# Output product of an attention stage: four half-precision products per 128 tokens, or two single-precision products of 64 tokens

## The chip, the cores and the metric

The kernel runs on one core of a Trainium2 chip. The metric is the device time of one execution in microseconds (us); the figure before the change is the median of three runs.

## The reference

The reference takes 16 sequences of 512 tokens of 128 channels. It normalizes each token (xn), and then computes two things from xn: a recurrent attention, and a mixture of eight experts with a shared expert beside them. The result is x + s * silu(g), where s is the attention's output and g the mixture's.

The attention has 16 heads of 8 channels. Tokens are mixed with their predecessors and projected to r, k and v. Within a chunk, y is the product of r and k of all earlier tokens, weighted with a decay, times v; from the chunks before comes r times a state that is carried on with k and v. Its last step is `out = y @ Wo.T + bo`, with Wo of 128 x 128: this is the product that is changed. Inputs, weights and outputs are single precision.

## The kernel before

The kernel has two long stages. The first normalizes, routes, computes the experts and the projections of r and k, and ends at about 555 us of the span. The second is the attention and the final gating.

The attention is worked off in 16 units (NA = 16). A unit `u` is 128 tokens of four sequences, so 512 columns, in two chunks of Q = 64 tokens (CH = 2) per sequence; a half `p` of a unit is two sequences. Every engine has a program of its own with a loop over `u`, written out by hand and skewed against the others: in one turn of the loop the engine works on unit `u` for one step and on `u - 1` or `u - 2` for another. Semaphores tie them together, and each engine takes its instructions in order.

TensorE (PE) in one turn (lines 1743 to 1760): `pe_local` of the second half of `u - 1` (r times k, L1672), `pe_inter` of `u - 1` (state times r, L1652), `pe_av` of its first half (L1693), `pe_out` of `u - 2` (the output product, L1704 to L1707), `pe_kv` and `pe_local` of `u` in three pieces (L1614, L1616, L1621 and L1672), `pe_av` of the second half of `u - 1` (L1693), and `pe_update` of `u` (k times v for the state, L1636).

VectorE (DVE) in one turn: `dve_select` gathers y of a half from the result of `pe_av` and adds the part of the state (L1321, four instructions a half), `dve_state` carries the state on (L1292, two a unit), and `dve_decay` weights r times k (L1303, four a unit). The selected y stands in `y32` in single precision; its columns are ordered by half, chunk, sequence and token.

The output product takes half-precision operands. For that y is split. `act_high` on ScalarE (ACT) rounds a half of `y32` to `yh` (L864), and `pool_low` on GpSimd (POOL) computes `yl = y32 - yh` (L670); for the last unit VectorE does this (`dve_low_last`, L1338). Both also put the columns in plain token order. The weights Wo stand as a pair, too, in slot 6 of `wph` and `wpl`. `pe_out` waits for `y_lo` (both low halves of the unit) and for the state of unit `u + 1`, since it writes to a PSUM bank that the update of the state also uses. Then, for each of four blocks of 128 tokens, it adds four products of 128 x 128: the bias (`f2y` times `brw`), `yh` with the high weights, `yh` with the low weights, and `yl` with the high weights. The last unit goes through `pe_out_last`, by halves, and its gating (L1345) and final sum (L1352) are done on VectorE, behind the gating of the unit before (L1330).

GpSimd's turn begins with the two `pool_low`; behind them stand a mask of the state (L663) for unit `u + 2`, the final sum of `u - 2` (L698), two additions of the experts' rows (L677, L682), the gating (L688), and the mask for unit `u + 1`, which `pe_inter` waits for. ScalarE's turn holds `act_high` of the first half behind the copies of k and v (L843), and of the second half between the masks of r (L857) and the weighting of the experts' rows (L872).

Before `dve_select` overwrites `y32` of unit `u - 2`, it waits for its low halves (`y_lo`).

Of the kernel before, what the change touches and what calls it, by code (L numbers as in the profile page):

```python
# [7 lines left out]
F32, F16, I32 = mybir.dt.float32, mybir.dt.float16, mybir.dt.int32  # L8
ALU = mybir.AluOpType
# [3 lines left out]
P = 128  # L13
HEADS, HD = 16, 8
Q = 64
CH = P // Q
GROUP = 32
GROUPS = P // GROUP
HPG = GROUP // HD
# [11 lines left out]
SW = 2.0 ** 8  # L31
# [38 lines left out]
def build(nc, nb, x, decay, per_head, maa, wT, bias, bias_rows, gateT, w1e, w3e, w2e, w1s, w3s, w2s, const, out):  # L70
# [8 lines left out]
    NA = TPS * NG  # L79
# [9 lines left out]
    with ctx:  # L89
        def sb(name, shape, dt=F32):  # L90
            return ctx.enter_context(nc.sbuf_tensor(name, shape, dt))
# [28 lines left out]
        sem = Semaphores()  # L120
# [19 lines left out]
        take = carve(ffn[:, 0:NT // 2, :].rearrange("p a b -> p (a b)"))  # L140
# [20 lines left out]
        take = carve(hidden[:, :])  # L161
# [63 lines left out]
        mx = sb("mx", [P, 3])  # L225
        omx = sb("omx", [P, 3])
        w32 = late([P, 4, P])
        ws32 = late([P, 7, P])
        wph = sb("wph", [P, 7, P], F16)
        wpl = sb("wpl", [P, 7, P], F16)  # L230
        brk = sb("brk", [P, 2])
        brs = sb("brs", [P, 2])
        bro = late([P, 3 * P])
# [29 lines left out]
        a32 = take([P, 2, GROUPS, 2 * HPG * Q])  # L263
        yint = take([P, 2, 512])
        y32 = take([P, 2, 512])
        yh = take([P, 2, 512], F16)
        yl = take([P, 2, 512], F16)
        st = [first_state, take([P, NG, 4 * HALF])]
        sm = take([P, 4, 4 * HALF])
        picked = [take([P, PRING, 4, P]) for k in range(2)]  # L270
# [83 lines left out]
            v = a[:, 4 * g * TPS:4 * (g + 1) * TPS]  # L354
            return v.rearrange("p (b t) d -> p b t d", t=TPS)[:, :, tt, :]

        def by_chunk(a, u, p):
            return a[:, u % 2, 2 * p * P:2 * (p + 1) * P].rearrange("p (c b i) -> p b c i", c=CH, b=2)

        def in_order(a, u, p):  # L360
            return a[:, u % 2, 2 * p * P:2 * (p + 1) * P].rearrange("p (b c i) -> p b c i", c=CH, b=2)

        NHOTS = 2 * NT
        HOT_FIRST, HOT_SLOTS, HOT_LAG = 13, 24, 3
# [64 lines left out]
        def at(u):  # L429
            return 0 <= u < NA  # L430
# [173 lines left out]
        def pool_program(e):  # L604
# [59 lines left out]
                                st[c][:, g, :].rearrange("p (b d) -> p b d", b=4),  # L664
                                rep_mid(C("head"), 4), ALU.mult).then_inc(sem[f"masked{c}"], 1)

            def pool_low(n):
                u, p = divmod(n, 2)
                G.wait_ge(sem["y_hi"], n + 1)
                G.tensor_tensor(in_order(yl, u, p), by_chunk(y32, u, p), in_order(yh, u, p), ALU.subtract).then_inc(sem["y_lo"], 1)  # L670

            def pool_add(u, step):
                p0 = picked[0][:, u % PRING, :, :]
                if step == 0:
# [37 lines left out]
                    pool_scatter(q - SCATTER_LAG)  # L712
            pool_state0()
            for u in range(-2, NA + 3):
                if at(u - 1) and u - 1 < NA - 1:
                    pool_low(2 * (u - 1))
                    pool_low(2 * (u - 1) + 1)
                if at(u + 2):
                    pool_mask(2 * (u + 2))
                if at(u - 2) and u - 2 < NA - 3:  # L720
                    pool_end(u - 2)
                if at(u):
                    pool_add(u, 0)
                    pool_add(u, 1)
                if at(u - 1) and u - 1 < NA - 2:
                    pool_gate(u - 1)
                if at(u + 1):
                    pool_mask(2 * (u + 1) + 1)
                if u - 1 in (NA - 3, NA - 2):
                    pool_end(u - 1)  # L730

        @block.scalar
        def act_program(e):
# [122 lines left out]
                    A.wait_ge(sem["local"], 2 * (u - 1))  # L856
                A.mul(rm[:, u % 2, q, :], r32[:, u % RRING, :], C("slot")[:, q:q + 1]).then_inc(sem[f"rmask{q // 2 * 2}"], 1)  # L857

            def act_high(n):
                u, p = divmod(n, 2)  # L860
                A.wait_ge(sem["ysel"], HPG * (n + 1))
                if u >= 2 and p == 0:
                    A.wait_ge(sem["s_out"], u - 1)
                A.copy(in_order(yh, u, p), by_chunk(y32, u, p)).then_inc(sem["y_hi"], 1)  # L864

            def act_weigh(u, k):
                A.wait_ge(sem[f"picked{u % PRING}"], 32 * (u // PRING + 1))
                if u == 0:
# [54 lines left out]
            for u in range(-2, NA + 3):  # L923
                if at(u - 1):
                    act_weigh(u - 1, 0)
                if at(u - 2) and u - 2 < NA - 2:
                    act_out(u - 2)
                if at(u):
                    act_kv(u, 0)
                    act_kv(u, 1)  # L930
                if at(u - 1):
                    act_high(2 * (u - 1))
# [8 lines left out]
                if at(u - 1):  # L941
                    act_high(2 * (u - 1) + 1)
                if at(u):
                    act_weigh(u, 1)
                    act_inter(u)

        @block.vector
        def dve_program(e):
# [298 lines left out]
            def dve_proj_weights(i):  # L1247

                if i == 1:
                    V.wait_ge(sem["late_in"], 48)  # L1250
                    V.wait_ge(sem["mixes"], 1)
                    V.tensor_scalar(ws32[:, 6, :], w32[:, 3, :], SW, None, ALU.mult).then_inc(sem["aconst"], 1)
                V.tensor_scalar(ws32[:, i, :], w32[:, i, :], omx[:, i:i + 1], SW, ALU.mult, ALU.mult).then_inc(sem["aconst"], 1)
                V.tensor_scalar(ws32[:, 3 + i, :], w32[:, i, :], mx[:, i:i + 1], SW, ALU.mult, ALU.mult).then_inc(sem["aconst"], 1)

            def dve_proj_pair(step):

                V.wait_ge(sem["aconst"], 8 + 2 * step)
                for some in (slice(1, 3), slice(4, 7)):
                    if step == 0:  # L1260
                        V.tensor_copy(wph[:, some, :], ws32[:, some, :]).then_inc(sem["aconst"], 1)
                    else:
                        V.tensor_tensor(wpl[:, some, :], ws32[:, some, :], wph[:, some, :], ALU.subtract).then_inc(sem["aconst"], 1)
# [41 lines left out]
            def dve_select(n, heads):  # L1305
                u, p = divmod(n, 2)
                if heads[0] == 0:
                    V.wait_ge(sem["av"], n + 1)
                    V.wait_ge(sem["yint"], u + 1)
                    if u >= 2 and p == 0:  # L1310
                        V.wait_ge(sem["y_lo"], 2 * (u - 1))

                def pair(a):
                    return a[:, u % 2, 2 * p * P:2 * (p + 1) * P].rearrange("p (a i) -> p a i", i=Q)

                for q in heads:
                    if q > 0:
                        V.wait_ge(sem["ysel"], HPG * n + q)
                    first = av_bank(n)
                    y = banks[:, first:first + 2, :].rearrange("p c (b q i) -> p (c b) q i", b=2, q=HPG)[:, :, q, :]  # L1320
                    V.scalar_tensor_tensor(pair(y32), y, C("slot_y")[:, q:q + 1], pair(y32 if q else yint),  # L1321
                                           ALU.mult, ALU.add).then_inc(sem["ysel"], 1)

            def dve_gate(u):
# [8 lines left out]
            def dve_low_last(p):  # L1333
                u = NA - 1
                V.wait_ge(sem["y_hi"], 2 * u + p + 1)
                if p == 0:
                    V.wait_ge(sem["s_out"], u - 1)
                V.tensor_tensor(in_order(yl, u, p), by_chunk(y32, u, p), in_order(yh, u, p), ALU.subtract).then_inc(sem["y_lo_last"], 1)  # L1338

            def dve_gate_last(p):  # L1340
                V.wait_ge(sem["out_last"], p + 1)
# [84 lines left out]
            for u in range(-2, NA + 3):  # L1426
# [11 lines left out]
                if at(u + 2):  # L1438
                    dve_decay(2 * (u + 2), 1)
                    dve_decay(2 * (u + 2), 0)  # L1440
            for p in range(2):
                dve_low_last(p)
            dve_gate(NA - 2)
            for p in range(2):
                dve_gate_last(p)
# [3 lines left out]
        def pe_program(e):  # L1449
# [245 lines left out]
                k.then_inc(sem["av"], 1)  # L1695

            def pe_out(u):
                T.wait_ge(sem["y_lo"], 2 * (u + 1))
                T.wait_ge(sem["state"], 2 * (u + 2))
                s = u % 2  # L1700
                for b in range(4):
                    o = psum[1][:, b * P:(b + 1) * P]
                    X = slice(b * P, (b + 1) * P)
                    T.matmul(o, f2y[:, :], brw[:, 2 * P:3 * P], start=True, stop=False)  # L1704
                    T.matmul(o, yh[:, s, X], wph[:, 6, :], start=False, stop=False)
                    T.matmul(o, yh[:, s, X], wpl[:, 6, :], start=False, stop=False)
                    k = T.matmul(o, yl[:, s, X], wph[:, 6, :], start=False, stop=True)  # L1707
                k.then_inc(sem["s_out"], 1)

            def pe_out_last(p):  # L1710
                T.wait_ge(sem["y_lo_last"], p + 1)
                s = (NA - 1) % 2
                for b in range(2):
                    o = psum[4 + p][:, b * P:(b + 1) * P]
                    X = slice((2 * p + b) * P, (2 * p + b + 1) * P)
                    T.matmul(o, f2y[:, :], brw[:, 2 * P:3 * P], start=True, stop=False)
                    T.matmul(o, yh[:, s, X], wph[:, 6, :], start=False, stop=False)
                    T.matmul(o, yh[:, s, X], wpl[:, 6, :], start=False, stop=False)
                    k = T.matmul(o, yl[:, s, X], wph[:, 6, :], start=False, stop=True)
                k.then_inc(sem["out_last"], 1)  # L1720

            for b in range(nb + 2):
# [67 lines left out]
```

## Time and profile before

| what | value |
|---|---|
| median of three runs | 721.59 us (720.73 to 722.53) |
| span of the profiled execution, from its first to its last instruction | 719.3 us |
| TensorE busy | 654.1 us, 91% |
| VectorE busy | 555.4 us, 77% |
| ScalarE busy | 494.9 us, 69% |
| GpSimd busy | 478.9 us, 67% |
| attention stage | from about 555 us to the end of the span |

The profiled execution's own time is known by its span alone: 719.3 us, from its first to its last instruction; the median of the timed runs stands 2.3 us above it. Busy shares are means over both stages. The start of a matmul is recorded and its end is modelled, so a matmul that overlaps the one before it counts as busy twice over; the rows below are read by starts.

### The profile page before, as it was taken

To read this page: it belongs to the slowest core of one execution; us is meant where nothing else is said; L and a number is where in the kernel's file an instruction comes from. 1 tells how busy PE (TensorE), PEld (TensorE's weight loads), DVE (VectorE), ACT (ScalarE), POOL (GpSimd) and SP (SyncE) were. 2 spreads that over 40 slices of the span, in tenths; PEclk is the share of its full clock that TensorE was granted. 3 is DMA by queue.
4 is the path that set the end of the run, shared out by engine and by line. 5 is a ranking of instruction groups with operands and counts; after the bars stand their busy time and mean duration, and the time that the engine had idled before them with its cause. 6 is when DMAs were issued, how large, how long until landed. Compare 5 with 4: busy or idle time off the path is not lost.

```text
span 719.3 us, 22370 instructions
## 1 busy us (share of the span) xinstructions
PE 654.1 (91%) x8536; PEld 452.1 (63%) x8536; DVE 555.4 (77%) x1058; ACT 494.9 (69%) x1008; POOL 478.9 (67%) x519
## 2 busy tenths in 40 slices
PE   2787897978999999999999999999997899999993
PEld 1544565646665665566666666878886676777772
DVE  5989986877667886667766676667664899999996
ACT  4864798857665656666666666666665788888872
POOL 4844321244777777777777777767778487888873
PEclk9999999999999999999999999999999999999997
DMA  9931111111111323433323334333362767777762
GB/s 243 299 95 45 45 61 46 45 51 36 48 49 49 108 91 108 137 108 108 110 92 109 106 106 139 110 101 108 97 103 93 237 179 230 216 229 222 233 176 59
DMA packets 88616, 86.75 MB, mean 121 GB/s; under 512 B 11394, under 2 KB 65284, under 8 KB 88516
## 3 DMA queue, kind: packets, MB, share of 16 engines
q1 hardware_dynamic: 79428, 66.70, 29.8%
q0 software_dynamic: 9088, 18.63, 9.6%
q8 instruction: 73, 1.20, 0.7%
q14 instruction: 27, 0.22, 0.1%
HBM read 50.82 MB, written 34.47 MB: 119 GB/s over the span
## 4 chain that ended last, share of the span: by engine, by line
PE 53%; DVE 13%; ACT 12%; POOL 11%; issue 7%; DMA 3%; SPq 0%; POOLq 0%; DVEq 0%; ACTq 0%
PE banks L1556 7%; PE banks L1558 7%; PE banks L1557 7%; PE banks L1596 5%; DVE hidden L1218 4%; POOL expert_rows L644 4%; PE banks L1576 4%; PE banks L1577 4%; PE banks L1575 4%; POOL srows L634 3%; ACT hidden L785 3%; PE banks L1621 3%; PE banks L1693 3%; PE banks L1672 3%; ACT rows L823 2%
## 5 line engine op out<-in xcount | busy, mean ns | idle before, releaser
L785 ACT CAST hidden<-hidden 128x512 f16<-128x512 f32 x206 | 127.1, 617 | 135.5 <-DVE hidden L1218 135.4
L634 POOL DMA_INDIRECT srows<-normed_rows,source x142 | 149.7, 1054 | 60.4 <-issue 40.2
L1222 DVE TENSOR_TENSOR hidden<-hidden 128x512 f16<-128x512 f32 x180 | 124.4, 691 | 83.9 <-ACT hidden L785 83.0
L1218 DVE TENSOR_TENSOR hidden<-hidden,banks 128x512 f32<-128x512 f32 x206 | 140.8, 684 | 44.0 <-ACT hidden L781 38.2
L1575 PE MATMUL banks<-wwords,hidden 128*128 (+1 forms) x824 | 148.8, 219 | 1.5 <-DVE hidden L1222 1.1
L1576 PE MATMUL banks<-wwords,hidden 128*128 (+1 forms) x824 | 148.6, 219 | 0.0
L1577 PE MATMUL banks<-wwords,hidden 128*128 (+1 forms) x824 | 148.6, 219 | 0.0
L781 ACT ACTIVATE hidden<-banks 128x512 f32<-128x512 f32 x206 | 122.7, 596 | 28.1 <-PE banks L1558 27.8
L1556 PE MATMUL banks<-sx,wwords 128*128 128x512 f16 (+1 forms) x368 | 121.5, 330 | 3.2 <-DVE wwords L1013 2.7
L1558 PE MATMUL banks<-sx,wwords 128*128 128x512 f16 (+1 forms) x368 | 121.6, 330 | 0.0
L1557 PE MATMUL banks<-sx,wwords 128*128 128x512 f16 (+1 forms) x368 | 121.5, 330 | 0.0
L644 POOL DMA_INDIRECT expert_rows<-ybuf,dest x72 | 77.2, 1072 | 22.8 <-issue 19.8
L1575 PEld LDWEIGHTS banks<-wwords,hidden 128*128 128x128 f16 x824 | 80.6, 98 | 12.4 <-issue 2.0
L644 POOL DMA_INDIRECT expert_rows<-rows,dest x70 | 72.8, 1040 | 23.1 <-issue 20.1
L1576 PEld LDWEIGHTS banks<-wwords,hidden 128*128 128x128 f16 x824 | 80.6, 98 | 11.3
L624 POOL TENSOR_TENSOR hidden<-hidden 128x512 f16<-128x512 f32 x26 | 33.6, 1294 | 76.8 <-ACT hidden L785 76.8
L1303 DVE TENSOR_TENSOR wwords<-banks,wmat 128x1024 f32<-128x1024 f32 x64 | 75.3, 1217 | 10.9 <-PE banks L1672 10.5
L1577 PEld LDWEIGHTS banks<-wwords,hidden 128*128 128x128 f16 x824 | 80.6, 98 | 0.0
L1556 PE MATMUL banks<-xh,wwords 128*128 128x512 f16 x128 | 49.2, 385 | 19.1 <-DVE hidden L1218 18.7
L1321 DVE SCALAR_TENSOR_TENSOR hidden<-banks,cst,hidden 128x256 f32<-128x256 f32 x128 | 61.5, 481 | 3.8 <-ACT hidden L849 0.7
L1558 PEld LDWEIGHTS banks<-sx,wwords 128*128 x368 | 36.0, 98 | 25.6
L1557 PE MATMUL banks<-xl,wwords 128*128 128x512 f16 x128 | 49.0, 383 | 0.0
(218 smaller groups left out, 1429.7 us busy)
## 6 DMA issues: line engine op xcount, KB each, us to landing
rows<-x SPq DMA_DIRECT2D x32, 256.0 KB, 4.9
rows<-expert_rows SPq DMA_DIRECT2D x32, 256.0 KB, 3.6
normed_rows<-rows SPq DMA_DIRECT2D x16, 256.0 KB, 3.9
r_rows<-rows SPq DMA_DIRECT2D x16, 256.0 KB, 2.1
rd_rows<-rows SPq DMA_DIRECT2D x16, 256.0 KB, 2.2
stage<-r_rows SPq DMA_DIRECT2D x16, 256.0 KB, 4.0
k_rows<-rows SPq DMA_DIRECT2D x16, 256.0 KB, 2.2
kd_rows<-rows SPq DMA_DIRECT2D x16, 256.0 KB, 2.2
```

The source lines that it names most:

```text
L634: G.indirect_dma_start(srows[:, q % NXB, t, :], None, rows_in, bass.IndirectOffsetOnAxis(source[:, at:at + 1], 0)).then_inc(sem[f"s_in{q % ...
L644: G.indirect_dma_start(rows_out, bass.IndirectOffsetOnAxis(dest[:, at:at + 1], 0), ring_of(q)[:, t, :], None).then_inc(sem[f"y_stored{q % ...
L781: A.activation(sg[:, i % 2, :], psum[2 * (i % 2)][:, :], ACT.Silu, scale=1.0 / SW).then_inc(sem["silu"], 1)
L785: A.copy(guh[:, i % 4, :], gu[:, i % 2, :]).then_inc(sem["gu_hi"], 1)
L1218: V.tensor_tensor(gu[:, i % 2, :], sg[:, i % 2, :], psum[2 * (i % 2) + 1][:, :], ALU.mult).then_inc(sem["gated"], 1)
L1222: V.tensor_tensor(gul[:, i % 4, :], gu[:, i % 2, :], guh[:, i % 4, :], ALU.subtract).then_inc(sem["gu_lo"], 1)
L1556: T.matmul(o, a, mh, start=True, stop=False)
L1557: T.matmul(o, a, ml, start=False, stop=False)
L1558: k = T.matmul(o, b, mh, start=False, stop=True)
L1575: T.matmul(o, guh[:, i % 4, s], a, start=(j == 0 and n == 0), stop=False)
L1576: T.matmul(o, guh[:, i % 4, s], b, start=False, stop=False)
L1577: k = T.matmul(o, gul[:, i % 4, s], a, start=False, stop=last)
```

## The change

The pair of y is gone: `yh` and `yl`, `act_high`, `pool_low` and `dve_low_last` with their places in the three loops, and slot 6 of `wph` and `wpl`. `pe_out` waits for the selections of y themselves (`ysel`), and takes `y32` and single-precision weights `wo32`. In a block of 128 tokens the bias is added as before, and then two products follow, each with 64 columns of `y32` (one chunk of one sequence) as the stationary operand and the 128 columns of `wo32` as the moving one; the first writes partitions 0 to 63 of the block's result, the second partitions 64 to 127. `dve_select` waits for the output product of unit `u - 2` (`s_out`) in place of its low halves.

```diff
-        wph = sb("wph", [P, 7, P], F16)
-        wpl = sb("wpl", [P, 7, P], F16)
+        wph = sb("wph", [P, 6, P], F16)
+        wpl = sb("wpl", [P, 6, P], F16)
+        wo32 = sb("wo32", [P, P])
...
+        def piece(a, u, b, c):
+            at = b // 2 * 2 * P + c * P + b % 2 * Q
+            return a[:, u % 2, at:at + Q]
...
-            def pool_low(n):
-                u, p = divmod(n, 2)
-                G.wait_ge(sem["y_hi"], n + 1)
-                G.tensor_tensor(in_order(yl, u, p), by_chunk(y32, u, p), in_order(yh, u, p), ALU.subtract).then_inc(sem["y_lo"], 1)
...
-            def act_high(n):
-                u, p = divmod(n, 2)
-                A.wait_ge(sem["ysel"], HPG * (n + 1))
-                if u >= 2 and p == 0:
-                    A.wait_ge(sem["s_out"], u - 1)
-                A.copy(in_order(yh, u, p), by_chunk(y32, u, p)).then_inc(sem["y_hi"], 1)
...
-                    V.tensor_scalar(ws32[:, 6, :], w32[:, 3, :], SW, None, ALU.mult).then_inc(sem["aconst"], 1)
+                    V.tensor_scalar(wo32[:, :], w32[:, 3, :], SW, None, ALU.mult).then_inc(sem["aconst"], 1)
...
-                for some in (slice(1, 3), slice(4, 7)):
+                for some in (slice(1, 3), slice(4, 6)):
...
-                        V.wait_ge(sem["y_lo"], 2 * (u - 1))
+                        V.wait_ge(sem["s_out"], u - 1)
...
-            for p in range(2):
-                dve_low_last(p)
...
             def pe_out(u):
-                T.wait_ge(sem["y_lo"], 2 * (u + 1))
+                T.wait_ge(sem["ysel"], HPG * 2 * (u + 1))
                 T.wait_ge(sem["state"], 2 * (u + 2))
-                s = u % 2
                 for b in range(4):
                     o = psum[1][:, b * P:(b + 1) * P]
-                    X = slice(b * P, (b + 1) * P)
                     T.matmul(o, f2y[:, :], brw[:, 2 * P:3 * P], start=True, stop=False)
-                    T.matmul(o, yh[:, s, X], wph[:, 6, :], start=False, stop=False)
-                    T.matmul(o, yh[:, s, X], wpl[:, 6, :], start=False, stop=False)
-                    k = T.matmul(o, yl[:, s, X], wph[:, 6, :], start=False, stop=True)
+                    for c in range(CH):
+                        k = T.matmul(o[c * Q:(c + 1) * Q, :], piece(y32, u, b, c), wo32[:, :], start=False, stop=True)
                 k.then_inc(sem["s_out"], 1)
```

`pe_out_last` is changed in the same way, and waits for the selections of its half.

## Rows read from the trace of the kernel before

**Rows 1.** Stretches: two units' length; PE, PEld, DVE, ACT, POOL busy, clock, DMA.
```profile
core 0: us, PE busy (x) PEld busy (x) DVE busy (x) ACT busy (x) POOL busy (x), PEclk, DMA share, GB/s
634.76:644.10 9.34, 9.20 (x255) 6.77 (x248) 9.09 (x16) 7.94 (x20) 7.77 (x9) 1.00 0.73 215
644.10:653.44 9.34, 9.20 (x255) 6.77 (x248) 9.09 (x16) 7.95 (x20) 7.77 (x9) 1.00 0.82 244
```

**Rows 2.** Waits of VectorE, 572 to 700 us: total, times, longest.
```profile
DVE wwords L1303 <- PE banks L1672: 1.2, 3, 0.6
DVE hidden L1321 <- PE banks L1693: 0.2, 1, 0.2
DVE hidden L1292 <- PE banks L1636: 0.2, 1, 0.2
```

**Rows 3.** Timeline of one turn: start, length, instruction, count, idle before.
```profile
645.02 1.52 DVE L1321 SCALAR_TENSOR_TENSOR hidden<-banks,cst,hidden 128x256 f32<-128x256 f32 x3
645.50 1.15 PE L1652 MATMUL banks<-wwords,rows 64*64 64x64 f32 x32
646.45 0.47 DVE L1292 SCALAR_TENSOR_TENSOR stage<-hidden,ws,banks 128x256 f32<-128x256 f32 x1
646.68 1.10 PE L1693 MATMUL banks<-wwords 64*32 64x256 f32 x32
646.68 0.39 ACT L864 CAST wwords<-hidden 128x256 f16<-128x256 f32 x1
647.15 0.68 POOL L670 TENSOR_TENSOR hidden<-hidden,wwords 128x256 f16<-128x256 f32 x1 [0.61 <-ACT wwords L864]
647.89 0.23 PE L1704 MATMUL banks<-brw,f2y 128*128 128x128 f16 x1
647.95 0.22 PE L1705 MATMUL banks<-wph,wwords 128*128 128x128 f16 x1
...
648.79 0.32 PE L1614 MATMUL banks<-cst,wwords 128*128 128x128 f32 x1
...
649.34 0.28 PE L1614 MATMUL banks<-cst,wwords 128*128 128x128 f32 x1
649.45 0.22 PE L1616 MATMUL banks<-brw,f 128*128 128x128 f16 x1
...
649.73 0.22 PE L1621 MATMUL banks<-wpl,xh 128*128 128x128 f16 x1
649.79 0.22 PE L1621 MATMUL banks<-wph,xl 128*128 128x128 f16 x1
649.94 1.12 PE L1672 MATMUL banks<-wwords,rows 32*64 32x256 f32 x32
650.99 0.33 PE L1614 MATMUL banks<-cst,wwords 128*128 128x128 f32 x1
...
652.14 1.09 PE L1693 MATMUL banks<-wwords 64*32 64x256 f32 x32
653.17 0.69 PE L1636 MATMUL banks<-wwords 64*64 64x64 f32 x32
653.79 1.12 PE L1672 MATMUL banks<-wwords,rows 32*64 32x256 f32 x32
```

**Rows 4.** Groups of instructions, 572 to 704 us: count, busy, mean ns, idle before.
```profile
L1704 PE MATMUL banks<-brw,f2y 128*128 128x128 f16 x56 | 12.4, 222 | 1.2
```

**Rows 5.** Timeline of TensorE where L1652 begins: its first pair, then two pairs.
```profile
645.50 0.27 PE L1652 MATMUL banks<-wwords,rows 64*64 64x64 f32 x2
...
645.50 0.33 PE L1652 MATMUL banks<-wwords,rows 64*64 64x64 f32 x4
```

**Rows 6.** Timeline of TensorE ahead of one other output product.
```profile
589.85 1.55 PE L1693 MATMUL banks<-wwords 64*32 64x256 f32 x32
591.33 0.23 PE L1704 MATMUL banks<-brw,f2y 128*128 128x128 f16 x1
```

**Rows 7.** Timeline of VectorE at the end of the span.
```profile
705.42 3.98 DVE L1321 SCALAR_TENSOR_TENSOR hidden<-banks,cst,hidden 128x256 f32<-128x256 f32 x8
709.32 0.98 DVE L1338 TENSOR_TENSOR hidden<-hidden,wwords 128x256 f16<-128x256 f32 x2
710.22 0.68 DVE L1330 SCALAR_TENSOR_TENSOR rows<-banks,rows 128x512 f32<-128x512 f32 x1
```

**Rows 8.** Stretches at the end of the span, columns as in rows 1.
```profile
700.00:710.00 10.00, 6.36 (x188) 4.33 (x180) 9.53 (x19) 5.29 (x15) 6.29 (x7) 0.95 0.19 54
710.00:719.30 9.30, 1.68 (x16) 1.41 (x14) 3.25 (x6) 0.00 (x0) 1.26 (x1) 0.50 0.20 56
```

More of the change, by code:

```diff
@@ L227, in build @@
         w32 = late([P, 4, P])
-        ws32 = late([P, 7, P])
-        wph = sb("wph", [P, 7, P], F16)
-        wpl = sb("wpl", [P, 7, P], F16)
+        ws32 = late([P, 6, P])
+        wph = sb("wph", [P, 6, P], F16)
+        wpl = sb("wpl", [P, 6, P], F16)
+        wo32 = sb("wo32", [P, P])
         brk = sb("brk", [P, 2])
@@ L265, in build @@
         y32 = take([P, 2, 512])
-        yh = take([P, 2, 512], F16)
-        yl = take([P, 2, 512], F16)
         st = [first_state, take([P, NG, 4 * HALF])]
@@ L714, in pool_program @@
             for u in range(-2, NA + 3):
-                if at(u - 1) and u - 1 < NA - 1:
-                    pool_low(2 * (u - 1))
-                    pool_low(2 * (u - 1) + 1)
                 if at(u + 2):
@@ L930, in act_program @@
                     act_kv(u, 1)
-                if at(u - 1):
-                    act_high(2 * (u - 1))
                 if at(u + 1):
@@ L940, in act_program @@
                     act_mask(u + 1, 1)
-                if at(u - 1):
-                    act_high(2 * (u - 1) + 1)
                 if at(u):
@@ L1331, in dve_gate @@
                                        ALU.mult, ALU.mult).then_inc(sem["s_read"], 1)
[L1333 to L1338, printed above, removed]
             def dve_gate_last(p):
@@ L1697, in pe_out @@
             def pe_out(u):
-                T.wait_ge(sem["y_lo"], 2 * (u + 1))
+                T.wait_ge(sem["ysel"], HPG * 2 * (u + 1))
                 T.wait_ge(sem["state"], 2 * (u + 2))
-                s = u % 2
                 for b in range(4):
                     o = psum[1][:, b * P:(b + 1) * P]
-                    X = slice(b * P, (b + 1) * P)
                     T.matmul(o, f2y[:, :], brw[:, 2 * P:3 * P], start=True, stop=False)
-                    T.matmul(o, yh[:, s, X], wph[:, 6, :], start=False, stop=False)
-                    T.matmul(o, yh[:, s, X], wpl[:, 6, :], start=False, stop=False)
-                    k = T.matmul(o, yl[:, s, X], wph[:, 6, :], start=False, stop=True)
+                    for c in range(CH):
+                        k = T.matmul(o[c * Q:(c + 1) * Q, :], piece(y32, u, b, c), wo32[:, :], start=False, stop=True)
                 k.then_inc(sem["s_out"], 1)
             def pe_out_last(p):
-                T.wait_ge(sem["y_lo_last"], p + 1)
-                s = (NA - 1) % 2
+                T.wait_ge(sem["ysel"], HPG * (2 * NA - 1 + p))
                 for b in range(2):
                     o = psum[4 + p][:, b * P:(b + 1) * P]
-                    X = slice((2 * p + b) * P, (2 * p + b + 1) * P)
                     T.matmul(o, f2y[:, :], brw[:, 2 * P:3 * P], start=True, stop=False)
-                    T.matmul(o, yh[:, s, X], wph[:, 6, :], start=False, stop=False)
-                    T.matmul(o, yh[:, s, X], wpl[:, 6, :], start=False, stop=False)
-                    k = T.matmul(o, yl[:, s, X], wph[:, 6, :], start=False, stop=True)
+                    for c in range(CH):
+                        k = T.matmul(o[c * Q:(c + 1) * Q, :], piece(y32, NA - 1, 2 * p + b, c), wo32[:, :], start=False, stop=True)
                 k.then_inc(sem["out_last"], 1)
```

4 lines of the change are left out of this document (removed).

## The prediction

> **What bounds the kernel now.** The change touches the attention stage alone, so the page's shares (TensorE 91%) say little. I read the stage first by stretches of one turn, then the waits, then a timeline of one turn. By stretches a turn takes 9.34 us, with TensorE busy for 9.20 and VectorE for 9.09; ScalarE (7.95) and GpSimd (7.77) have room [rows 1]. Two engines are full. The waits of VectorE from 572 to 700 us add up to 1.6 us, all in a few turns [rows 2]: in the steady turns it goes from one instruction to the next, and its own work is 9.34 us long. So VectorE sets the turn, and TensorE has almost the same length.
>
> How much room TensorE has is in the timeline [rows 3], read by starts. In a run of 128 x 128 half-precision matmuls the next starts 0.06 after the last (649.73, 649.79), that is 0.16 before the modelled end of the last (0.22 long). Wherever the form of the array changes, the next starts only 0.07 before that end: L1621 ends at 650.01 and L1672 starts at 649.94; L1672 ends at 651.06, L1614 starts at 650.99; L1693 ends at 653.23, L1636 starts at 653.17; L1636 ends at 653.86, L1672 starts at 653.79. So a change of form costs 0.09 us, also where only the columns change (64*32 to 64*64, L1693 to L1636). Two places are later than that. L1693 starts at 646.68, 0.03 after the end of L1652 (646.65), so 0.10 late; it waits for VectorE's L1321, done at 646.54. L1704 starts at 647.89, 0.11 after the end of L1693 (647.78), so 0.18 late: it waits for the second low half on GpSimd (L670, done at 647.83), which waited for ScalarE's L864. These 0.28 us are TensorE's whole room: its work is 9.06 us a turn.
>
> **The change, part by part.** The output product now takes 0.90 us: 16 matmuls, from 647.89 to the next L1614 at 648.79 [rows 3]. The new one has 12 matmuls, but of two forms: four blocks of one 128 x 128 bias product and two single-precision products with 64 stationary columns. The trace has no single-precision product over all 128 rows with 64 columns, so I build its cost from neighbours.
>
> The columns: a single-precision L1614 of 128 columns holds the engine from 649.34 to 649.45, 0.11 us, twice a half-precision one [rows 3]. The tiled ones agree: a pair of L1652 with 64 columns takes 0.06 [rows 5]. I take 0.11 for 128 columns; the upper bound is twice that, since no row shows a real product over 128 rows. The Trainium skill speaks for that bound: in "FP8 and Floating Point Precision", section "TensorE Precision Notes", a true single-precision product takes four passes through the array. The products on tiles here take two column times, so the trace does not bear the rule out for them; by the rule each block would cost 0.11 us more.
>
> The two halves: the pair of L1652 starts together (645.50, two within 0.27) on separate tiles [rows 5]. The new pair shares all rows and takes separate columns. Lower bound 0.11 for both, upper bound 0.22. I take 0.11: the 32 matmuls of L1672, of 256 columns on tiles of 32*64, take 1.12 us [rows 3]. Four rounds of eight, at 0.22 a round, leave 0.24 for a load and the pipeline; if only the four row groups ran together, eight rounds would be 1.76 alone. So two matmuls that share their rows did run side by side.
>
> The change of form: into 64 columns and back again, two a block. Lower bound 0, if the form goes by rows alone; upper bound 0.09 each. I take 0.09, since L1693 to L1636, with the same rows, pays it [rows 3].
>
> The stationary load: behind a change it is not hidden. The first pair of L1652 is 0.27 long, where 0.16 and its 0.06 would be 0.22, so 0.05 [rows 5]; for the bias product it is within the 0.06 from L1704 to L1705 [rows 3].
>
> A block is then 0.07 (bias, with its load) + 0.09 (change) + 0.05 (load) + 0.12 (both products, the second started 0.01 later) + 0.09 (change back) = 0.42; four make 1.68 us. That is 0.78 more than now.
>
> What goes from the path: the 0.18 us that L1704 waits for GpSimd. What is late next is not y: the last selection is done at 646.54, and the other semaphore (L1292) at 646.92, both before TensorE is through with L1693 at 647.78 [rows 3]. So the 0.18 goes entirely.
>
> Per turn TensorE takes 0.78 - 0.18 = 0.60 us more. Its work plus the 0.10 wait on VectorE (which follows from the update through L1292 and L1321 and stays) becomes 9.94 us, above VectorE's 9.34: TensorE sets the turn, and the 0.60 counts in full. There are 14 output products from 572 to 704 us (L1704 x56, four each) [rows 4]. Three of them did not wait for GpSimd; the shape is that of the one at 591.33, where L1693 took 1.55 us and ended at 591.40, 0.07 after L1704's start [rows 6]. The product of the unit before the last lies in that turn beside VectorE's long last stretch and costs nothing. Sum: 14 x 0.78 - 11 x 0.18 = 10.9 - 2.0 = +8.9 us.
>
> At the end VectorE loses the two L1338. Behind the last L1321, L1330 starts at 710.22, where L1338 starts now, at 709.32 [rows 7]: -0.9 us. The last products take 0.84 us a half at the rate above; from 710 us on the granted clock is 0.50, the lower of the two levels (1.2 GHz), behind a stretch in which TensorE was busy for 6.36 of 10 us [rows 8], and there it would be 1.7. The first half's can start with its own selections, two us before the second's, and the second's runs while VectorE does L1330 and the first half's gating, so I count nothing for them.
>
> At nothing I cost: L864 and L670 themselves (ScalarE and GpSimd have 1.4 and 1.6 us of room a turn [rows 1], and if they had none their loss could only help); the new wait of VectorE for `s_out` of two units earlier, which is done a turn before (behind that wait stand the four L1321 of the half and the next L1303); and the shorter conversions of weights, two instructions once, in the first stage.
>
> Together +8.0 us: the span goes from 719.3 to 727.3. The median of the runs lies 2.3 us above the span, and I carry that over: 721.6 + 8.0 = 729.6 us.
>
> **The rivals.**
>
> Changing the columns alone is free with all rows in use, and the halves run together. Then the product takes 4 x (0.06 + 0.12) = 0.72 us, TensorE falls to 8.9 us a turn and VectorE's 9.34 decides. What is to be had is the end's 0.9 us and at most VectorE's 1.6 us of waiting: 719.1 to 720.7, say 719.9 us, not slower. If the halves run one after the other, it is 1.12 us, and TensorE comes 0.04 us a turn above VectorE's length: 721.6 + 0.6 - 0.9 = 721.3. It decides up to a product of 1.08 us (0.90 now and the 0.18 that it no longer waits). For it: no row shows this form. Against it: every change in the turn costs the same 0.09, that of columns too. The page "TensorEngine Tiling (Array Packing)" of the Trainium skill has a change of mode drain the array ("Key Properties") and lists 128 x 64 as a mode of its own ("Available Configurations"); by that rule the change is paid for and this rival falls. Chance 0.16.
>
> The halves do not overlap, or single precision over 128 rows takes four column times. Each adds 0.11 a block, 14 x 4 x 0.11 = 6.2 us: 735.8 us. For the first: no pair in the trace shares all its rows. For the second: no single-precision product over 128 rows stands in the trace, only transposes (L1614). Against both: the tiles of 32*64 and 64*64 [rows 3, 5]. The second is the rule of four passes above. Chance 0.11 and 0.07; with both, 742 us, 0.02.
>
> The load or a change is partly hidden, or a long L1693 like the 1.55 us of [rows 6] comes more often or less: 724 to 728, or 731 to 733. I count it with the forecast.
>
> **How the numbers follow.** Forecast 729.6 with 0.64, its own range 724 to 733; free changes 0.16; a dearer product 0.20. A time within 0.3% (719.4 to 723.8) can't be told from no change. Faster by more needs nearly all of VectorE's waiting and the end: 0.07. Within: the rest of the first rival and a small cost, 0.12. Slower: 0.81. The range 721.0 to 736.5 holds the forecast, the dearer products but for both at once, and the upper part of the first rival.
>
> **What would show it.** A turn of 9.9 us, from one update of the state to the next; VectorE idle for 0.6 us a turn, waiting for TensorE; from the first bias matmul to L1614 1.68 us, with 0.15 from each bias product to the first half, 0.01 to the second, and 0.25 from there to the next bias product; L1693's end and the first bias matmul 0.07 apart as at the other changes; L1330 right behind the last L1321. Wrong it would be if bias and halves follow each other within 0.06 to 0.12, if VectorE is still without gaps, or if the second half starts 0.1 behind the first.

## The result, and the profile after

The changed kernel takes 735.86 us (median of 4 runs, 733.87 to 737.35). The kernel before took 722.06 us beside it (4 runs, 720.73 to 722.61). The ratio is 1.018, with a 95% interval of 1.015 to 1.021: slower by about 14 us, where 8 were forecast. The time lies in the predicted range (721.0 to 736.5) near its upper end, and within 0.1 us of what the dearer-product rival gave (735.8). The profiled execution has a span of 734.2 us, against 719.3 before.

The first view is the stage by turns, with the columns of [rows 1]: two turns of the kernel after.

```profile
core 0: us, PE busy (x) PEld busy (x) DVE busy (x) ACT busy (x) POOL busy (x), PEclk, DMA share, GB/s
632.56:642.95 10.39, 10.36 (x253) 7.01 (x245) 9.08 (x15) 7.56 (x18) 6.47 (x6) 1.00 0.68 201
642.95:653.34 10.39, 10.36 (x252) 7.07 (x244) 9.06 (x15) 7.54 (x18) 6.48 (x6) 1.00 0.71 210
```

A turn is 10.39 us instead of 9.34. VectorE does the same work as before (9.08 us busy), TensorE fills the turn, and its granted clock is 1.00, so nothing here is a matter of the clock. The waits of VectorE from 572 to 716 us answer to [rows 2] (total, times, longest):

```profile
DVE wwords L1281 <- PE banks L1641: 15.4, 14, 1.3
```

There is now one listed wait in each of the 14 turns that hold an output product, 1.1 us long on the mean: `dve_decay` (L1281, before L1303) waits for `pe_local` (L1641, before L1672). TensorE sets the turn. The two ends of one such wait, from the timelines of TensorE and VectorE:

```profile
650.13 1.12 PE L1641 MATMUL banks<-wwords,rows 32*64 32x256 f32 x32
651.36 2.36 DVE L1281 TENSOR_TENSOR wwords<-banks,wmat 128x1024 f32<-128x1024 f32 x2 [1.11 <-PE banks L1641]
```

`dve_decay` begins 0.11 us behind the modelled end of `pe_local` (650.13 + 1.12 = 651.25). What fills TensorE's turn is in the timeline of TensorE around one output product, the counterpart of [rows 3] (start, length, instruction, count):

```profile
645.80 1.12 PE L1662 MATMUL banks<-wwords 64*32 64x256 f32 x32
646.86 0.23 PE L1671 MATMUL banks<-brw,f2y 128*128 128x128 f16 x1
647.02 0.44 PE L1673 MATMUL banks<-wo,hidden 128*64 128x128 f32 x4
647.39 0.23 PE L1671 MATMUL banks<-brw,f2y 128*128 128x128 f16 x1
647.55 0.44 PE L1673 MATMUL banks<-wo,hidden 128*64 128x128 f32 x4
...
648.98 0.33 PE L1583 MATMUL banks<-cst,wwords 128*128 128x128 f32 x1
```

The bias product (L1671) starts 0.06 ahead of the modelled end of `pe_av` (L1662: 645.80 + 1.12 = 646.92), so the wait for GpSimd is gone. From there to the next bias product are 0.53 us, and to `pe_kv` (L1583) 2.12 us. The count behind the halves is the point: `x4` in each block, where the code calls two products. A narrower window of the same timeline ends between the first pair of records and the second:

```profile
647.02 0.33 PE L1673 MATMUL banks<-wo,hidden 128*64 128x128 f32 x2
```

The groups of TensorE over the whole span, by form, say the same (count, then busy us and mean ns of one, then idle before):

```profile
L1641 PE MATMUL banks<-wwords,rows 32*64 32x256 f32 x1024 | 37.1, 395 | 0.0
...
L1673 PE MATMUL banks<-wo,hidden 128*64 128x128 f32 x240 | 26.4, 298 | 0.0
L1583 PE MATMUL banks<-cst,wwords 128*128 128x128 f32 x64 | 19.8, 309 | 5.4 <-DMA wwords<-kd_rows 5.4
L1671 PE MATMUL banks<-brw,f2y 128*128 128x128 f16 x60 | 13.8, 229 | 0.0
```

L1671 is called four times in each of 15 units, 60 times, and has 60 records. L1673 is called eight times a unit, 120 times, and has 240. L1583 is a transpose in single precision, four a unit in 16 units: 64 calls, 64 records. And `pe_local` makes 16 calls a half, 512 in all, and has 1024 records. So each true single-precision product stands in the trace as two matmuls of two column times each, and a single-precision transpose as one.

At the end of the span VectorE goes from the last selection (L1299, before L1321) straight to the gating (L1308, before L1330), as [rows 7] would without the two L1338:

```profile
721.21 3.98 DVE L1299 SCALAR_TENSOR_TENSOR hidden<-banks,cst,hidden 128x256 f32<-128x256 f32 x8
725.11 0.68 DVE L1308 SCALAR_TENSOR_TENSOR rows<-banks,rows 128x512 f32<-128x512 f32 x1
```

The balance takes the start of the first and last update of the state as its marks. These are the first and last group of L1605 after, then of L1636 before:

```profile
559.47 0.69 PE L1605 MATMUL banks<-wwords 64*64 64x64 f32 x32 [0.68 <-ACT wwords L832]
...
715.94 0.69 PE L1605 MATMUL banks<-wwords 64*64 64x64 f32 x32
```

```profile
557.24 0.69 PE L1636 MATMUL banks<-wwords 64*64 64x64 f32 x32 [0.68 <-ACT wwords L843]
...
700.15 0.69 PE L1636 MATMUL banks<-wwords 64*64 64x64 f32 x32
```

From the first to the last update the time grows from 142.9 to 156.5 us, by 13.6. From the last update to the end of the span it falls from 19.1 to 18.2, by 0.9. The first update comes 2.2 us later. That last part is not the change: in the other profiles of this study, where the first stage is the same but for the weights' conversion, it lies anywhere from 556.7 to 560.1 us.

### The profile page after: what moved, and what is told of

Its sections match the earlier page's. It is cut to its first block, busy times and chain, and to the rows that moved or that the text cites. A ratio compares the mean times of both kernels' runs of the same rounds, so it can differ in the third digit from the quotient of the medians.

```text
span 734.2 us, 22419 instructions
## 1 busy us (share of the span) xinstructions
PE 673.5 (92%) x8600; PEld 457.0 (62%) x8600; DVE 554.2 (75%) x1056; ACT 488.0 (66%) x976; POOL 461.7 (63%) x489
## 4 chain that ended last, share of the span: by engine, by line
PE 46%; POOL 19%; DVE 12%; issue 9%; ACT 9%; DMA 3%; SPq 0%; DVEq 0%; POOLq 0%; ACTq 0%
POOL expert_rows L641 10%; POOL srows L631 9%; PE banks L1525 5%; PE banks L1527 4%; PE banks L1526 4%; PE banks L1662 4%; PE banks L1641 4%; DVE hidden L1196 4%; PE banks L1565 3%; PE banks L1673 3%; ACT hidden L774 3%; PE banks L1590 3%; PE banks L1621 2%; PE banks L1545 2%; PE banks L1546 2%
## 5 line engine op out<-in xcount | busy, mean ns | idle before, releaser
L1281 DVE TENSOR_TENSOR wwords<-banks,wmat 128x1024 f32<-128x1024 f32 x64 | 75.2, 1217 | 25.6 <-PE banks L1641 25.6
L1299 DVE SCALAR_TENSOR_TENSOR hidden<-banks,cst,hidden 128x256 f32<-128x256 f32 x128 | 61.4, 480 | 3.2 <-issue 0.3
```

## The experiments

A turn below is the steady distance between two updates of the state, and "the product" the time from the first bias product to the start of `pe_kv`. Kernels named together ran together, with the kernel before as their common base.

### The parts of the new product (e1 to e4; before: 721.84 us, 20 runs)

**The bias in one product ahead of the others.** One product of 512 columns in place of four, so that the form changes twice a unit and not eight times.

```diff
+                T.matmul(psum[1].rearrange("p (b d) -> p b d", b=4), f2y[:, :], rep_mid(brw[:, 2 * P:3 * P], 4), start=True, stop=True)
                 for b in range(4):
...
-                    T.matmul(o, f2y[:, :], brw[:, 2 * P:3 * P], start=True, stop=False)
                     for c in range(CH):
...
```

> The changed kernel, with the bias of all four blocks in one 128 x 128 product of 512 columns ahead of the eight single-precision products: two changes of form a unit in place of eight. Theory (a single-precision product is issued as two matmuls of two column times each, 0.21 us for 128 columns, and a change of form costs 0.09 and an exposed load 0.05): a unit's product takes 0.22 + 0.09 + 0.05 + 8 x 0.11 + 0.09 = 1.33 us in place of 2.12, a turn 9.60 in place of 10.39, 14 turns -11 us: 725 us. Rival (single precision costs two column times as predicted, and the 6 us beyond the prediction are dearer changes of form, about 0.15 each): the product falls below 1.1, VectorE's 9.34 a turn decides, 721 us. Rival (the time lies outside the output product): no change, 736 us.

725.38 us (723.81 to 727.37, 5 runs), ratio 1.0052 (1.0029 to 1.0074); a turn of 9.61 us. The timeline of TensorE:

```profile
661.30 0.39 PE L1669 MATMUL banks<-brw,f2y 128*128 128x512 f16 x1
661.62 1.09 PE L1673 MATMUL banks<-wo,hidden 128*64 128x128 f32 x16
662.65 0.33 PE L1583 MATMUL banks<-cst,wwords 128*128 128x128 f32 x1
```

The product takes 1.35 us, 0.77 less than the change as made. Six changes of form and the stationary loads that they lay bare are gone, and the columns are the same. The 16 records take 1.03 us up to `pe_kv`. Without the change back (0.09) and the first load (0.05) that is 0.22 for each of the four pairs of calls, not the 0.12 of the prediction.

**The bias in 64-column pieces.** The form never changes inside the product; the bias takes eight matmuls for four.

```diff
-                    T.matmul(o, f2y[:, :], brw[:, 2 * P:3 * P], start=True, stop=False)
+                    for c in range(CH):
+                        T.matmul(o[c * Q:(c + 1) * Q, :], f2y[:, 0:Q], brw[:, 2 * P:3 * P], start=True, stop=False)
```

> The changed kernel, with the bias added in the 64-column form too, as two half-precision products a block: no change of form within the output product, four more matmuls. Theory (two matmuls a product, changes at 0.09): 0.05 + 4 x 0.06 + 8 x 0.11 + 0.09 = 1.26 us in place of 2.12, a turn of 9.53, 14 turns -12 us: 724 us, still above the kernel before. Rival (dearer changes of form alone): VectorE's turn of 9.34, 721 us. Rival (outside the product): 736 us.

723.48 us (722.61 to 726.11, 8 runs), ratio 1.0029 (1.0014 to 1.0044); a turn of 9.49 us, a product of 1.23.

```profile
659.02 0.25 PE L1672 MATMUL banks<-brw,f2y 128*64 128x128 f16 x2
659.10 0.39 PE L1674 MATMUL banks<-wo,hidden 128*64 128x128 f32 x4
659.32 0.22 PE L1672 MATMUL banks<-brw,f2y 128*64 128x128 f16 x2
...
660.25 0.33 PE L1583 MATMUL banks<-cst,wwords 128*128 128x128 f32 x1
```

Within one form the bias pair takes 0.08 us and a pair of single-precision products 0.22; a block is 0.30 instead of 0.53. The 0.23 between them is what two changes and one exposed load cost.

**Half-precision operands in the same places.** The forms and the changes stay, and the two products of a block take half-precision columns of the normalized input and a projection's weights. So y is left out of the result.

```diff
-                        k = T.matmul(o[c * Q:(c + 1) * Q, :], piece(y32, u, b, c), wo32[:, :], start=False, stop=True)
+                        k = T.matmul(o[c * Q:(c + 1) * Q, :], xh[:, (4 * b + c) * Q:(4 * b + c + 1) * Q], wph[:, 0, :], start=False, stop=True)
```

> The changed kernel with half-precision operands in the same two products of 64 columns a block (other data: columns of the normalized input times a projection's weights, so y is left out of the result); forms, changes and waits stay. Theory (the excess is single precision, two matmuls of two column times): a block falls from 0.53 to 0.07 + 0.09 + 0.05 + 0.06 + 0.09 = 0.37, the product to 1.47, a turn to 9.74, 14 turns -9 us: 727 us. Rival (dearer changes): only one of two column times goes, 0.05 a block, -3 us: 733 us.

724.48 us (723.18 to 726.82, 6 runs), ratio 1.0042 (1.0020 to 1.0064); a turn of 9.62 us.

```profile
658.68 0.23 PE L1671 MATMUL banks<-brw,f2y 128*128 128x128 f16 x1
658.84 0.25 PE L1673 MATMUL banks<-wph,xh 128*64 128x128 f16 x2
659.02 0.23 PE L1671 MATMUL banks<-brw,f2y 128*128 128x128 f16 x1
...
660.03 0.33 PE L1583 MATMUL banks<-cst,wwords 128*128 128x128 f32 x1
```

Now the trace has two records a block (`x2`), one for each call, side by side within 0.25 us, and a block takes 0.34 us instead of 0.53. The 0.16 from bias to halves is the same, so it is the form that costs it and not the precision. The size was expected at 0.37 a block. The 0.03 less fits a shorter load: from a half-precision pair to the next bias are 0.18 us, where one pass (0.06), the second half's start (0.01) and a change (0.09) make 0.16. That leaves some 0.02 for a load of 64 half-precision columns against 0.05 for a single-precision one, an inference from these two rows.

**The new product without its bias.** What is left is one form and 16 records.

```diff
-                    T.matmul(o, f2y[:, :], brw[:, 2 * P:3 * P], start=True, stop=False)
                     for c in range(CH):
-                        k = T.matmul(o[c * Q:(c + 1) * Q, :], piece(y32, u, b, c), wo32[:, :], start=False, stop=True)
+                        k = T.matmul(o[c * Q:(c + 1) * Q, :], piece(y32, u, b, c), wo32[:, :], start=True, stop=True)
```

> The changed kernel without the bias product: the bias is left out of the result, and the output product has one form. Theory: 0.05 + 8 x 0.11 + 0.09 = 1.02 us, TensorE's turn would be 9.29, so VectorE decides with 9.34 and shows no gaps: 14 x -1.05 = -15 us, 721 us, about the kernel before less the 0.9 us at the end. If TensorE decided all the same, the turn would be 9.29 with gaps on VectorE. Rival (outside the product): 736 us.

720.92 us (719.01 to 724.99, 10 runs), ratio 0.9985 (0.9966 to 1.0003); a turn of 9.29 us. From the timelines of TensorE and VectorE:

```profile
648.72 1.09 PE L1672 MATMUL banks<-wo,hidden 128*64 128x128 f32 x16
649.74 0.33 PE L1583 MATMUL banks<-cst,wwords 128*128 128x128 f32 x1
...
650.90 1.12 PE L1641 MATMUL banks<-wwords,rows 32*64 32x256 f32 x32
...
652.12 2.36 DVE L1281 TENSOR_TENSOR wwords<-banks,wmat 128x1024 f32<-128x1024 f32 x2
```

The product takes 1.02 us, as expected. The turn is 9.29 us and not VectorE's 9.34, which was the sign named for TensorE deciding all the same. The steady turns list no wait of VectorE, but the starts show one: L1281 begins 0.10 behind the modelled end of L1641 (650.90 + 1.12 = 652.02), as close as in the kernel after, where it is seen waiting for it. So TensorE sets this turn too, and VectorE alone needs no more than 9.29.

### What the kernel before could gain (e5 to e8; before: 721.32 us, 21 runs)

**The new product for the last unit only.** The kernel before, with y in single precision in `pe_out_last` alone (its bias in one product); VectorE loses the two L1338, and ScalarE the last unit's two roundings.

```diff
-            for p in range(2):
-                dve_low_last(p)
...
-                T.wait_ge(sem["y_lo_last"], p + 1)
+                T.wait_ge(sem["ysel"], HPG * (2 * NA - 1 + p))
...
+                    for c in range(CH):
+                        k = T.matmul(o[c * Q:(c + 1) * Q, :], piece(y32, NA - 1, 2 * p + b, c), wo32[:, :], start=False, stop=True, skip_group_check=True)
```

> The kernel before, with the new product for the last unit alone: two single-precision products a block behind one bias product of 256 columns, and no low halves on VectorE at the end; the other 15 units keep the half-precision pair. Theory: turns stay at 9.34, from the last update of the state to the end 18.2 us in place of 19.1: -0.9 us, 721 us. Rival (the end is set by the stores, not by VectorE): no change at the end, 721.8 us.

720.59 us (718.29 to 726.35, 12 runs), ratio 0.9998 (0.9979 to 1.0017). The turns stay at 9.34 us, and from the last update to the end are 18.2 us instead of 19.1: the 0.9 is in the trace, but a time with this spread doesn't show it.

**The old product one step later.** The kernel before, with `pe_kv(u, 0)` ahead of `pe_out(u - 2)`, so that the low half of y has time to be ready.

```diff
+                if at(u):
+                    pe_kv(u, 0)
                 if at(u - 2):
                     pe_out(u - 2)
...
-                    pe_kv(u, 0)
```

> The kernel before, with the output product moved behind the first k and v product in TensorE's order, so that the low halves on GpSimd are done when it begins: it takes the 0.18 us wait away and leaves all work. Theory (VectorE sets the turn before the change): the wait goes, the turn stays within 0.05 of 9.34, 721 to 722 us. Rival (TensorE with its wait on GpSimd set the turn): 11 x 0.18 less, turns of 9.16, 720 us.

736.30 us (733.89 to 737.21, 5 runs), ratio 1.0200 (1.0180 to 1.0221); a turn of 10.41 us. Both theories missed. The waits of TensorE have a new row, 13 times a whole microsecond, and the timeline shows both ends of one of them:

```profile
PE banks L1614 <- ACT hidden L849: 13.0, 13, 1.0
```

```profile
657.08 0.56 ACT L849 COPY hidden<-banks 128x512 f32<-128x512 f32 x1
...
657.70 0.33 PE L1614 MATMUL banks<-cst,wwords 128*128 128x128 f32 x1 [1.00 <-ACT hidden L849]
...
658.76 0.22 PE L1704 MATMUL banks<-brw,f2y 128*128 128x128 f16 x1
```

L849 is ScalarE's copy of the state's part of y out of a PSUM bank, which `pe_kv` then writes. In the order of before, the output product stood in the time that this copy takes; moved, it left TensorE with nothing to do there. The output product's place covered ScalarE's work, and the experiment took the cover away together with the wait.

**Both of these edits.** The last unit's new product and the later `pe_out`.

> The two changes before together, as a version that might beat both kernels. Theory: -0.9 us from the end, and what TensorE's room gives back in turns where it stands still for other reasons: 720 to 721 us. Rival (the wait on GpSimd sets the turn): 719 us.

735.57 us (734.12 to 738.11, 5 runs), ratio 1.0200 (1.0178 to 1.0222), a turn of 10.41 us: a miss for the same reason.

**One single-precision product of 128 columns.** The kernel after, with the block's 128 columns of `y32` as they stand for one stationary operand, so half as many products. This is no replacement for the change: the tokens of a block don't stand side by side in `y32`, so the rows of the result come in another order.

```diff
-                    for c in range(CH):
-                        k = T.matmul(o[c * Q:(c + 1) * Q, :], piece(y32, u, b, c), wo32[:, :], start=False, stop=True)
+                    k = T.matmul(o, whole(y32, u, b), wo32[:, :], start=False, stop=True)
```

> The changed kernel with one single-precision product of 128 stationary columns a block in place of two of 64: no change of form at all. The stationary columns are taken as they lie (one chunk of two sequences), so the rows of the result come in another order. Theory (two matmuls of two column times a product, whatever its width): a block takes 0.06 + 0.22, the product 1.11 us, a turn 9.37 on TensorE against VectorE's 9.29 to 9.34: 721 to 722 us. Rival (the two-column-time matmul needs tiles of 64 columns, and the whole width takes four of them): 2.0 us, a turn of 10.26, 734 us.

722.68 us (721.91 to 724.84, 10 runs), ratio 1.0020 (1.0006 to 1.0033); a turn of 9.55 us, where 9.37 was expected: the product was priced at 1.11 us.

```profile
658.85 0.23 PE L1670 MATMUL banks<-brw,f2y 128*128 128x128 f16 x1
658.92 0.44 PE L1671 MATMUL banks<-wo,hidden 128*128 128x128 f32 x2
659.20 0.22 PE L1670 MATMUL banks<-brw,f2y 128*128 128x128 f16 x1
```

One call of 128 stationary columns is two records as well, one behind the other (0.33 and 0.11 more), so the count belongs to the precision and not to the 64 columns. The bias comes 0.07 ahead of it and not 0.16: with the same form there is no change. The four blocks take 1.34 us, 0.33 each against 0.53 with 64-column halves. That is 0.05 a block above the bias (0.06) and two records (0.22), which I put down to a load that is laid bare; no run takes that load by itself.

### Whether the wait for GpSimd cost the kernel before anything (e9, e10; before: 722.08 us, 23 runs)

**The wait in two.** The kernel before, with the first two blocks of `pe_out` waiting for the first low half only.

```diff
-                T.wait_ge(sem["y_lo"], 2 * (u + 1))
+                T.wait_ge(sem["y_lo"], 2 * u + 1)
...
                 for b in range(4):
+                    if b == 2:
+                        T.wait_ge(sem["y_lo"], 2 * (u + 1))
```

> The kernel before, with the output product's wait for the low halves split: blocks 0 and 1 wait for the first low half alone, blocks 2 and 3 for the second, so the first 0.45 us of the product lie over the last low half on GpSimd. Place and work of everything stay. Theory (VectorE sets the turn before the change): the 0.18 us wait goes, the turn stays at 9.29 to 9.34, and only turns in which VectorE waited for TensorE gain: 720.5 to 721.5 us. Rival (TensorE with its wait sets the turn): 11 turns of 9.16, 719.3 us.

721.55 us (720.44 to 723.30, 12 runs), ratio 0.9997 (0.9983 to 1.0012). The timeline, and a turn in the columns of [rows 1]:

```profile
647.34 1.10 PE L1693 MATMUL banks<-wwords 64*32 64x256 f32 x32
648.37 0.23 PE L1706 MATMUL banks<-brw,f2y 128*128 128x128 f16 x1
```

```profile
644.49:653.83 9.34, 9.31 (x249) 6.77 (x241) 9.08 (x15) 7.95 (x20) 7.77 (x9) 1.00 0.72 221
```

The first bias product (L1706 here) now starts 0.07 ahead of the end of L1693 and not 0.11 behind it [rows 3]: the wait in front of the product is gone, and the turn is 9.34 us as before. But TensorE gains nothing by it, for it waits as long at the product's end:

```profile
648.82 0.57 ACT L849 COPY hidden<-banks 128x512 f32<-128x512 f32 x1
649.22 0.22 PE L1709 MATMUL banks<-wph,hidden 128*128 128x128 f16 x1
649.44 0.33 PE L1614 MATMUL banks<-cst,wwords 128*128 128x128 f32 x1
```

L1614 follows the last half-precision product by 0.22 us, where 0.06 is usual, and begins 0.05 behind the end of ScalarE's copy (648.82 + 0.57 = 649.39). From the first bias product to L1614 are 1.07 us instead of 0.90. In the kernel before, the same copy ends at 648.73, also just ahead of L1614 at 648.79:

```profile
648.16 0.57 ACT L849 COPY hidden<-banks 128x512 f32<-128x512 f32 x1
```

So behind the wait for GpSimd stood another, for ScalarE, that is only some 0.01 us shorter. That is what the split could give back, and e9 doesn't show that TensorE's 0.18 us were free.

**The split wait and the new product for the last unit.** The parts of the study that cost nothing, together.

> The split wait together with the new product for the last unit alone, as the version that might beat both kernels. Theory: the 0.9 us at the end and what the split wait gives: 719.6 to 720.6 us. Rival (TensorE's wait sets the turn): 718.4 us.

720.17 us (718.55 to 725.20, 12 runs), ratio 0.9980 (0.9962 to 0.9998), a turn of 9.33 us and 18.2 us from the last update to the end. The end of VectorE has no L1338 any more (L1327 is the selection, L1336 the gating here):

```profile
706.07 3.98 DVE L1327 SCALAR_TENSOR_TENSOR hidden<-banks,cst,hidden 128x256 f32<-128x256 f32 x8
709.96 0.68 DVE L1336 SCALAR_TENSOR_TENSOR rows<-banks,rows 128x512 f32<-128x512 f32 x1
```

It is the one version with an interval below 1 against the kernel before, and only just: e5 has the same end and a ratio of 0.9998, and e9's edit leaves the turn as it was. By the two ratios (0.998 and 1.018) it is about 2% faster than the kernel after.

## Why the prediction came out as it did

**The step that failed: the size of the columns.** The prediction took "0.11 us for 128 columns" from L1614 [rows 3], which is a transpose, and named twice that as the upper bound "since no row shows a real product over 128 rows". The upper bound was the truth: two records of 0.11 a product, a block of 0.53 us and not 0.42, a product of 2.12 us and not 1.68. Over 14 units and four blocks that is 14 x 0.44 = 6.2 us, the rival's 6.2. The prediction gave that rival a chance of 0.07; the time lies in the range because the range was drawn to hold it too, while the forecast itself was 6.3 us low. The evidence against it in the prediction, L1672 and L1652, was misread: their records were taken for products. The 32 of L1672 are 16 calls of two records each, so the rows of the tiles, too, show two column times a record and four a product. That could have been seen ahead, by counting the calls in `pe_local` against the `x32`. e3 settles it: with half-precision operands in the same forms and places there is one record for each call, and 0.19 us a block go.

The rule of the Trainium skill that stood against the forecast, four passes for a true single-precision product ("FP8 and Floating Point Precision", section "TensorE Precision Notes"), agrees with these rows: 0.22 us for 128 columns is four times the 0.056 of a half-precision one. The prediction's remark that the trace does not bear it out for tiles was wrong.

**The two halves side by side: right.** In the narrow window the first two records of a block are 0.33 us long together, where one behind the other would need 0.11 more. That these are the two halves, and not the two records of one call, follows from e3, where each call has one record and the pair takes 0.25, and from e8, where the two records of one call come one behind the other. That rival is out, although its time was the same as that of the right one.

**The changes of form and the exposed load: right.** From the bias product to the first half are 0.16 us (0.15 predicted). e1 takes six changes and three loads away and saves 0.77 us a unit, near the 6 x 0.09 + 3 x 0.05 = 0.69 by the prediction's prices and the 0.05 by which one bias product of 512 columns (0.32 - 0.09 = 0.23) is shorter than four of 128 (4 x 0.07). The rule that a change of mode drains the array (the Trainium skill, "TensorEngine Tiling (Array Packing)", section "Key Properties") agrees with this, and the rival of the free column change falls with it: its 719.9 us would need a change at nothing.

**The wait for GpSimd, and the turn after the change: right.** L1671 follows L1662 as at any change of form, and the turn is 9.34 - 0.17 + 1.22 = 10.39 us, with TensorE the bound (0.17 is the wait by starts). VectorE's wait was predicted at 0.6 us and is 1.1; 0.44 of the difference is the term above.

**VectorE sets the turn before the change: not so, though the forecast didn't hang on it.** The prediction saw no wait of VectorE in the steady turns and took 9.34 us for its own work. There is one, too short for the list of waits:

```profile
651.17 2.35 DVE L1303 TENSOR_TENSOR wwords<-banks,wmat 128x1024 f32<-128x1024 f32 x2
```

L1672 ends at 651.06 [rows 3], and L1303 begins 0.11 behind it, as L1281 behind L1641 after the change. VectorE's own turn is 9.29 us at most (10.39 less the wait of 1.1, and e4). The turn of before goes through both engines: TensorE from L1693 to L1672, with the wait for GpSimd and the product, and VectorE from L1303 to the L1321 that L1693 waits for. So each turn follows the product: wait and product take 0.17 + 0.90 = 1.07 us at a turn of 9.34, and the product alone 1.02 at 9.29 (e4), 1.23 at 9.49 (e2), 1.35 at 9.61 (e1) and 2.12 at 10.39. e8 (1.34 at 9.55) is 0.06 below that line; 0.05 of it lies in the transposition right behind the product, whose successor starts 0.11 us after it there and 0.16 in the kernel after. For this reason what the product adds a turn counts in full, as the prediction had it. The remark on the first rival, that VectorE decides up to a product of 1.08 us, fails at e4.

**The end: right.** 0.9 us less from the last update on, in the profile after and in e5 and e10.

**The sum.** Between the updates the prediction has 14 x 0.78 - 11 x 0.18 = +8.9 us. The profile shows the product at 14 x 1.22 = +17.1, the wait gone in the 11 turns that had it at about 0.17 (-1.9), and some 1.7 us less because four turns of before, three of them those without that wait, stood still at other places (9.57 to 9.91 us long) more than those of after; together +13.5. With the end that is +12.6, and the medians differ by 13.8. The first stage, which varies by 3.4 us from profile to profile, is large enough to cover what is left. Why those turns of before were long was not tried.

## What to carry to other kernels

Before a row prices an operation that isn't in the trace, count its records against the calls in the code: here a single-precision product is two records and a transpose one, and a transpose is no price for a product. Each change between forms of the array cost about 0.09 us and laid a load bare, so products of one form are best put together: one bias product ahead of all (e1) gave back 0.77 of the 1.22 us that the new form adds. And before a step is moved to spare it a wait, look at what else its place covers: in e6 it was another engine's copy out of the bank that the next step needed, and in e9 the same copy stood 0.01 us behind the wait that was taken away. Last, an engine that lists no waits doesn't have to be the one that sets the turn: compare the start of its instruction with the end of what it needs, here 0.11 us apart both where a wait is listed and where none is.

## What was not expected of the hardware

- A single-precision product is two matmul records, whatever its form (e8: 128 columns; L1673: 64; L1641: tiles of 32 x 64); for every 128 moving columns each holds the engine for twice the 0.056 us that a half-precision product takes.
- A block of e8 changes no form and is still 0.05 us longer than its records; the blocks of e2, with 64 columns, are 0.02 longer than theirs (0.30 against 0.06 + 0.22). Loads are the likely cause, but that was not tried.
- The start of the attention stage varies by 3.4 us between executions with the same work ahead of it, more than the 0.9 us at the end that the change does give back.
